# Leaving out TensorE's products of the identity with itself in the prologue of an attention and feed-forward kernel

## The reference

```
x = x + _layernorm(_L0_attn_ref(_layernorm(x), qkv_w, conv_w0, conv_b0, conv_w1, conv_b1, proj_w, proj_b, ln_w, ln_b))
x = x + _layernorm(_L0_ffn_ref(_layernorm(x), w_gate, w_up, w_down, s_gate, s_up, s_down))

_L0_attn_ref:  qkv = tok @ qkv_w ; per branch: softmax(q k^T * scale) v + lepe(v)
               att = concat(x1, x2) @ proj_w + proj_b ; tok + norm(att) * ln_w + ln_b
_L0_ffn_ref:   gate = silu((x @ w_gate) * s_gate) ; up = (x @ w_up) * s_up
               ((gate * up) @ w_down) * s_down
```

## Time and profile before

| | |
|---|---|
| median of 3 runs | 1010.31 us (1009.2 to 1011.27) |
| the profiled execution, its own time | 1010.6 us |
| its span | 1008.9 us |
| mean granted TensorE clock | 0.959 |
| PE, DVE, POOL, ACT busy | 90%, 84%, 71%, 62% of the span |
| identity products (L724) | 40 entries in the trace, between 97.7 and 159.2 |

### The profile page before, as it was taken

One profiled execution on the slowest core, in us unless ns is written; L12 is line 12 of the kernel. 1 busy time (PEld: TensorE's weight loads), 2 busy tenths in 40 slices (PEclk: granted clock), 3 DMA queues, 4 the chain that ended last, 5 costly groups with the idle time before them and its releaser, 6 DMA issues. The chain is left out here.

```text
span 1008.9 us, 18469 instructions
## 1 busy us (share of the span) xinstructions
PE 909.3 (90%) x6503; PEld 707.5 (70%) x6503; DVE 852.0 (84%) x1270; ACT 624.6 (62%) x1058; POOL 720.0 (71%) x539
## 2 busy tenths in 40 slices
PE   3636628999999999999999999999999999999996
PEld 3424418777777777877777777777787777777773
DVE  6898898899999999999999999999999999353132
ACT  2745826867586767766686758676776665452431
POOL 3656656787779886997789876987699788542332
PEclk9866958999999999999999999999999999999998
DMA  6011050014102320114002310232011301120001
GB/s 179 0 43 42 1 125 1 1 42 114 34 2 64 84 64 0 33 48 111 16 0 62 98 48 0 62 83 62 1 25 53 76 17 63 54 52 2 22 1 42
DMA packets 78319, 46.14 MB, mean 46 GB/s; under 512 B 39608, under 2 KB 72376, under 8 KB 78264
## 3 DMA queue, kind: packets, MB, share of 16 engines
q1 hardware_dynamic: 73400, 45.10, 16.9%
q10 hardware_dynamic: 4864, 0.32, 0.3%
HBM read 28.63 MB, written 16.78 MB: 45 GB/s over the span
## 5 line engine op out<-in xcount | busy, mean ns | idle before, releaser
L1118 DVE TENSOR_TENSOR prod<-ps_x,qkvl 128x2048 f32<-128x2048 f32 x128 | 290.8, 2280 | 10.4 <-ACT ps_x L786 6.5
L650 PE MATMUL ps_gate<-xhi,wg 128*128 128x256 f16 x1024 | 230.6, 273 | 2.3 <-DVE xlo L1229 1.7
L650 PE MATMUL ps_gate<-xlo,wg 128*128 128x256 f16 x1024 | 230.5, 273 | 0.0
L650 PE MATMUL ps_up<-xhi,wu 128*128 128x256 f16 x1024 | 230.5, 273 | 0.0
L650 PE MATMUL ps_up<-xlo,wu 128*128 128x256 f16 x1024 | 230.5, 273 | 0.0
L856 ACT ACTIVATE gact<-ps_gate,sgate 128x256 f32<-128x256 f32 x256 | 106.6, 467 | 157.0 <-PE ps_gate L650 155.4
L1012 POOL TENSOR_TENSOR flo<-fuse,fhi 128x512 f16<-128x512 f32 x128 | 148.4, 1162 | 72.4 <-ACT fhi L862 72.3
L952 POOL TENSOR_TENSOR sum<-prod 128x1024 f32<-128x1024 f32 x64 | 150.6, 2364 | 39.9 <-DVE prod L1118 36.9
L1238 DVE SCALAR_TENSOR_TENSOR fuse<-ps_up,sup,gact 128x256 f32<-128x256 f32 x256 | 110.3, 472 | 75.8 <-PE ps_up L650 63.9
L961 POOL TENSOR_TENSOR sum<-prod 128x1024 f32<-128x1024 f32 x64 | 151.5, 2369 | 19.5 <-DVE prod L1118 12.8
L670 PE MATMUL ps_acc<-wd,flo 128*128 128x512 f16 x512 | 153.3, 379 | 0.0
(11 more groups left out here) (155 smaller groups left out, 1411.4 us busy)
## 6 DMA issues: line engine op xcount, KB each, us to landing
xb<-in_L_attn_x SPq DMA_DIRECT2D x64, 128.0 KB, 2.7
xr<-in_L_attn_x SPq DMA_DIRECT2D x16, 512.0 KB
attn_rows<-ratt SPq DMA_DIRECT2D x16, 512.0 KB, 3.5
o<-attn_rows SPq DMA_DIRECT2D x32, 256.0 KB, 4.2
out_x<-y SPq DMA_DIRECT2D x15, 512.0 KB
x<-in_L_ffn_w_gate SPq DMA_DIRECT2D x1, 1024.0 KB, 5.4
xr<-in_L_ffn_w_up SPq DMA_DIRECT2D x1, 1024.0 KB, 8.2
out_x<-y SPq DMA_DIRECT2D x2, 256.0 KB
```

The source lines that it names most:

```text
L650: mm = nc.tensor.matmul(ps[:, HALF * i:HALF * i + HALF], w[:, k, P * j:P * j + P], xs[:, k, rows], start=(k == 0 and part == 0), stop=(k = ...
L1118: nc.vector.tensor_tensor(prod[:, half].rearrange("p (s j k) -> p s j k", j=WIN, k=WIN), left[:, :, None, :].broadcast_to([P, 4 * WIN, WIN ...
```

## The change

The three steps are taken out of the list `BEFORE`, and their functions out of the PE program. With them go 4 + 8 + 8 products and two waits. No other engine's steps, waits or order are touched, and the result does not depend on the products.

```
-                  ("qkv", b, 0, 3), ("qx", b, 0), ("xt", b, 1, 1), ("warm", 0, 4), ("square", p, 0), ("pv", a, 3),
+                  ("qkv", b, 0, 3), ("qx", b, 0), ("xt", b, 1, 1), ("square", p, 0), ("pv", a, 3),
...
-                  ("norm1_add", 0), ("ffn_norm2", 0), ("attn_out", b), ("norm2_apply", 0), ("warm_fx", 0),
-                  ("warm_cat", a), ("pv_sum", b, 3), ("qk", c, 0), ("qk", c, 1), ("qx", c, 1), ("fx", 0, 0, 0),
+                  ("norm1_add", 0), ("ffn_norm2", 0), ("attn_out", b), ("norm2_apply", 0), 
+                  ("pv_sum", b, 3), ("qk", c, 0), ("qk", c, 1), ("qx", c, 1), ("fx", 0, 0, 0),
...
-            def warm(t, n, bank):
-                for _ in range(n):
-                    nc.tensor.matmul(ps_acc[1][:, 0:P], ident[:], ident[:], start=True, stop=True)
-
-            def warm_cat(at, bank):
-                pe.wait_ge(sum_done, 2 * UNITS * (2 * at[0] + at[1]) + 7)
-                warm(0, 8, bank)
-
-            def warm_fx(t, bank):
-                pe.wait_ge(f_stats, 2)
-                warm(0, 8, bank)
-
-            todo = {"warm": warm, "warm_cat": warm_cat, "warm_fx": warm_fx,
-                    "ln1_fin": ln1_fin, "xt": xt_step, "qkv": qkv, "cat": cat_step, "proj": proj, "fx": fx,
+            todo = {"ln1_fin": ln1_fin, "xt": xt_step, "qkv": qkv, "cat": cat_step, "proj": proj, "fx": fx,
```

## The result

The changed kernel took 1033.38 us (median of four executions; three lay between 1031.64 and 1034.41). The fourth, 1650.63 us at a mean granted clock of 0.558 where the others had 0.942 to 0.951, was in a slow state that is not explained here, and the ratio leaves it out. The kernel before took 1010.54 us beside it. The ratio is 1.0225, with a 95% interval of 1.0211 to 1.024. The forecast was 1011.2 us in a range of 1009.5 to 1012.9: wrong by 22 us.

What follows compares the result with a forecast made beforehand. PE was taken to set the pace from the first feed-forward product on. The terms -0.1 + 0.5 - 1.2 + 1.85 - 0.2 = +0.85 us, against the median of 1010.31, gave 1011.2 us, range 1009.5 to 1012.9.

Steps and rivals of the forecast that it cites:

- So the loop hands on a shift of PE's start almost one to one: Feed-forward loop: PE sets the pace, so a shift of its `gate` start passes on almost fully.
- the gain: End of the prologue: without the sixteen products `gate` starts at 160.5 in place of 161.72, 1.2 us gained.
- The cold start: First `gate` and `up` work: PE at half speed until the clock rises at 164.2; cost 1.85 us, bounds 1.1 and 2.6.
- The two waits for ACT: PE's later waits of 0.6 and 0.4 us shrink when PE comes late; -0.2 us, bounds 0 and -1.0.
- the fall at 103 to 105: Prologue without the four products: PE's longer idle gap before 103.51 may bring the clock down at 103 to 105.
- the -0.1: Four products at 97.71 out: `proj` behind them moves up, worth -0.1 us before DVE becomes the limit.
- The +0.5 us: Four products out: an earlier clock fall delays `proj` of slice (0,1) and DVE; +0.5 us, bounds 0 and +2.0.
- The rival of the full +2.0 us: The first four products held the clock up: +2.0 us at `cent_var` in place of +0.5, 1012.7 us; chance 0.15.
- The first: Rival: identity products were only in the way, the clock rises fast; -1.2 us, 1009.1 us; chance 0.17.
- The second: Rival: transposes don't count for the clock, so its rise counts from `gate`; +0.5 us more, 1011.7 us; chance 0.13.
- The third: Rival: the first four products held the clock up; +2.0 us at `cent_var` in place of +0.5, 1012.7 us; chance 0.15.
- The fourth: Rival: PE stays at 1.2 GHz well into the first chunks, until 166.9; 1012.5 us and up; chance 0.05.

Runs made afterwards that it cites:

- e2: Kernel before, all products in place, with the first instruction of PE's loop placed at slot 160 of a 256-instruction fetch block; 1023.98 us, ratio 1.0134.
- e4: Changed kernel with PE's loop head placed at slot 64 of a fetch block, no product put back; 1011.31 us, ratio 1.0007.
- e3: Changed kernel with PE's loop over four tiles written out, so no branch back on PE; 1011.22 us, ratio 1.0006.
- e9: Changed kernel with PE's loop head placed at slot 128 of a fetch block; 1021.75 us, ratio 1.0134.
- e6: Kernel before with only the four products taken out, the sixteen kept; 1010.64 us, ratio 1.0004.
- e7: Changed kernel with PE's loop head placed at slot 96 of a fetch block; 1011.56 us, ratio 1.001.
- e1: Changed kernel with twenty identity products put back at the start of PE's program, where nothing is waiting; 1012.0 us, ratio 1.0011.
- e11: Changed kernel, loop where it falls, with a branch prefetch hint for the closing branch of PE's loop; 1010.92 us, ratio 1.0005.
- e10: Changed kernel with PE's loop head placed at slot 224, near the end of its fetch block; 1026.37 us, ratio 1.0171.

## Why the prediction was wrong, point by point

**The step that failed** is the one that says "So the loop hands on a shift of PE's start almost one to one": the sum took each pass of the loop to run as before. Up to the first back-edge this held: PE's `cat` came at 378.06 in place of 376.57, 1.49 us later; 0.59 of that was there at ACT's L810 already and is no effect of the change, so 0.9 us were handed on. But the step put the turn of the loop at nothing. It had no term for where the loop lies in the program, and none of the rivals had one. The loop's passes lost 22 us at three back-edges (e2 and e4 show that the loop's place does it with or without the products; e3 that it takes a branch). The Trainium skill states this under "Runtime: NRT & Kernel Launch", Instruction fetch mechanics: instructions come in blocks of 16 KiB, 256 to a block, into a memory that holds 2048 on TensorE, and a taken branch to a block that isn't held waits for its fetch. The traces agree on the block (0.54 MB in 33 packets), on eight blocks held at once (2048 instructions), and on the wait, 2.8 to 3.3 us at a lost head, a time that the section doesn't give. The same section of the Trainium skill says that only the current two pages are held; the loop of 6.6 blocks that stayed for four passes, here with 33 packets in all, says otherwise for PE, and the measurement decides.

**The clock behind the prologue.** The forecast had it at 2.4 GHz from its rise on. At the first back-edge it came down within the wait of 3.3 us and stayed at 1.2 GHz for 10.2 us, through the second wait. Of the 22 us some 10 are this. It doesn't come with every such wait: in e2 it was 3.4 us at two of the three back-edges, and in e9 (waits of 2.8 to 3.0 us) none.

**The end of the prologue: right in its order.** Forecast against the changed kernel, each moment less the 0.6 us by which ACT's L810 came later: `fx` 156.2 against 156.15, its duration 2.1 against 1.97, `xlo` 158.63 against 158.5, `cat` 159.46 against 159.4, `gate` 160.5 against 160.3, so the gain was 1.4 us and not 1.2. The rise of the clock came later than the 164.2 that the forecast took. The stretch in which it lies in the changed kernel, and the one of e4, whose `gate` started at 159.69:

```profile
165.00:166.00 1.00, 1.00 (x8) 1.00 (x8) 1.00 (x1) 0.99 (x2) 0.00 (x0) 0.65 0.00 0
...
162.00:163.00 1.00, 1.00 (x8) 0.70 (x6) 1.00 (x1) 0.00 (x0) 1.00 (x1) 0.58 0.00 0
```

A mean of 0.65 puts it at 165.7, or 165.1 on the forecast's scale, within the bounds of 162.7 and 165.7. In the ten traces without the sixteen products the rise came 3.2 us (e4) to 4.8 us (the changed kernel) after the first `gate`, in nine of them 4.2 or more, where the forecast took 3.7. The cold start cost 1.6 to 2.4 us, mostly about 2.3, and not 1.85. The two waits for ACT that were to give back 0.2 us gave nothing; in the changed kernel the rows that answer to the earlier trace rows are

```profile
PE ps_gate L650 <- ACT gact L843: 0.6, 1, 0.6
PE ps_w L598 <- ACT xb L748: 0.4, 1, 0.4
```

**The four products: the fall at 103 to 105 did not come.** DVE's two `cent_var` in the changed kernel, which answer to the earlier trace rows:

```profile
101.83 1.22 DVE L1163 TENSOR_REDUCE cvar<-catt 128x64 f32<-128x1024 f32 x1
...
118.48 1.21 DVE L1163 TENSOR_REDUCE cvar<-catt 128x64 f32<-128x1024 f32 x1
```

Both come 0.6 us later than before, the second no more than the first, so nothing was lost or gained between them. PE's step at 104.09 took 1.10 us, the duration of full clock. The reading of what the products held up was wrong. PE in the kernel before, and then in the changed kernel:

```profile
98.66 0.38 PE L627 MATMUL ps_w<-bterm,evenly 96*128 96x512 bf16 x1
...
97.77 0.68 PE L598 MATMUL ps_w<-ident,xb 128*128 128x128 f32 x4 [0.78 <-ACT qkvl L764]
99.23 0.38 PE L627 MATMUL ps_w<-bterm,evenly 96*128 96x512 bf16 x1 [0.78 <-ACT xt L755]
```

Without the products `proj` waits 0.78 us for ACT's copy of `xt`, and less the 0.57 us of this execution it starts at 98.66, where it was. The four products had only filled this wait. So the -0.1 was nothing, PE's idle time before 104.09 is 1.71 us as it was 1.70 before 103.51 (and not 2.6), and the longer gap that was to bring the clock down never opened. The +0.5 us is too high too; e6 shows 1010.64 against 1010.41 us, nothing that can be told from zero. The rival of the full +2.0 us is out.

**The net of the products.** The forecast's +0.85 us can be read where the loop stays. Without the sixteen it took 1011.31, 1011.56, 1012.0, 1011.22 and 1010.92 us (e4, e7, e1, e3, e11), 0.4 to 1.2 us above the kernel before beside each; three of the five intervals include 1. The shift of 0.9 us at 378 is the most direct reading. The size fits, at the edge of what can be measured, but in part by luck: the terms for the four products (+0.4 together, measured as nothing) were too high, the cold start was mostly too low, by 0.3 to 0.6, and the gain and the waits for ACT were each off by 0.2 in opposite directions.

**The rivals.** The first (the products only in the way) is out by these same runs. The second, that transposes don't count for the clock, put the rise 4.7 us after `gate`, and 4.2 to 4.8 us in nine traces of ten is nearer to it than the 3.7 of the forecast; but the tenth has 3.2, and rises in the kernel before varied by 2 us, so what counts for the clock stays open. The third is out too: the fall that it needed before 105 did not come. The fourth had PE at 1.2 GHz in the first chunks until 166.9 or later; it did not happen there.

## What to carry to other kernels

An edit of a program changes more than its work: on the engine that sets the pace, count how many instructions lie ahead of a hardware loop and how many fetch blocks the loop touches, before and after. A loop that nearly fills the instruction memory should have its head placed, or its back-edge hinted, before small edits are timed, or each of them is timed with a chance of some 5 to 25 us on top (three back-edges here). In the profile, look at the instruction queue's packet count and at waits for "issue" at a loop's turn.

## What the runs showed of the hardware that was not expected

- A loop of 1687 instructions on PE stays at head slots 64 and 96 (and, by count, 41 and 57), is lost in three of nine executions at 111, and in every one at 128, 160 and 224.
- A lost back-edge costs one wait of 2.8 to 3.3 us (4.7 us in the one seen at slot 111). A second one follows where the rest of the head's block is done before some 3 us are over: 0.8 to 1.0 us at slot 233, 2.6 to 3.0 us at 249.
- With the branch hint, a loop that touches eight blocks needs no fetch at all after its first pass (32 packets in the whole execution), and the fetch of the block behind it, at 368.7 without the hint, doesn't happen.
- A branch over a gap, just ahead of a block's end, cost a wait of its own: 1.3 us at 270.36 in e10.
- The clock behind such waits can cost nearly as much as the waits, or nothing: 0.50 for 10.2, 6.8 and 6.8 us in the changed kernel, 1.00 throughout in e9.
